# ScalarE's order in the attention slots of a six-block decoder: one move, both exponentials, the other move

## The reference, cut to what matters

```
layer 0:  x = ln(x + attn0(x))                # softmax over a size-1 axis: no attention left
          x = ln(x + xattn0(x, ctx))          # 16 heads, causal, 3x3 filter on the scores  ("near")
          x = ln(x + ffn0(x))                 # MLA attention with rotary keys ("causal"), then 4 experts
layer 1:  x = ln(x + attn1(x))                # 16 heads, causal, plus a memory term          ("tally")
          x = ln(x + xattn1(x, ctx, indices)) # 16 heads over 64 gathered context tokens      ("count")
          x = ln(x + ffn1(x))                 # low-rank experts with running sums

each attention, per head:  s = q k^T (+ mask);  p = exp(s - rowmax(s));  out = (p / sum(p)) v
```

## Time and profile before

| | |
|---|---|
| median of 3 runs | 2637.9 us |
| profiled execution | 2646.27 us |
| its span | 2644.5 us |
| instructions | 38948 |
| granted TensorE clock, mean | 0.876 |
| TensorE busy | 2243.5 us (85%) |
| VectorE busy | 1341.9 us (51%) |
| ScalarE busy | 998.1 us (38%) |

### The profile page before, as it was taken

How to read it: one execution, slowest core, us unless ns; L and a number is a source line. 1 busy time by engine, 2 the same in 40 slices (tenths; PEclk the granted TensorE clock), 3 DMA queues, 4 the chain that set the end, 5 groups by cost and what they waited for, 6 DMA issues and landing times. The chain is left out here.

```text
span 2644.5 us, 38948 instructions
## 1 busy us (share of the span) xinstructions
PE 2243.5 (85%) x13569; PEld 1574.3 (60%) x13637; DVE 1341.9 (51%) x3927; ACT 998.1 (38%) x3145; POOL 363.0 (14%) x639
## 2 busy tenths in 40 slices
PE   8688898898889988896818588899999999999887
PEld 4356566666677755575704355566666666666655
DVE  7245455564645454322129466665656656566331
ACT  3133535343545443352202135453444444444220
POOL 2044141423232324001000000000000000000000
PEclk9768868877899998897958699998999999999888
DMA  8000000000232210344651000000000000000000
GB/s 296 9 4 1 5 5 9 9 5 9 94 104 83 80 31 29 114 162 172 231 135 48 14 10 1 10 5 5 10 5 10 5 10 5 6 5 5 5 1 9
DMA packets 50763, 116.27 MB, mean 44 GB/s; under 512 B 8192, under 2 KB 30464, under 8 KB 46976
## 3 DMA queue, kind: packets, MB, share of 16 engines
q1 hardware_dynamic: 49024, 109.49, 12.3%
q0 software_dynamic: 1536, 4.20, 0.5%
HBM read 90.20 MB, written 23.46 MB: 43 GB/s over the span
## 5 line engine op out<-in xcount | busy, mean ns | idle before, releaser
L690 ACT ACTIVATE PRS<-PT 128x384 f32<-128x384 f32 (+1 forms) x512 | 265.6, 519 | 847.0 <-PE PT L621 846.4
L753 DVE TENSOR_REDUCE negmax<-SM 128x2 f32<-128x512 f32 x432 | 283.9, 687 | 229.1 <-PE SM L584 121.8
L621 PE MATMUL PT<-const_sb,PRS 128*128 128x128 f32 x1664 | 314.2, 307 | 40.0 <-ACT PRS L690 33.9
L705 ACT ACTIVATE PRS<-SM,negmax 128x128 f32<-128x128 f32 x608 | 248.3, 423 | 142.6 <-DVE negmax L753 142.6
L621 PEld LDWEIGHTS PT<-const_sb,PRS 128*128 128x128 f32 x1664 | 210.1, 155 | 134.9 <-issue 101.4
L2756 DVE TENSOR_SCALAR arena<-arena 128x256 bf16<-128x256 bf16 x1024 | 210.5, 281 | 9.2 <-PE SC L2774 8.2
L574 PE MATMUL SM<-haloU,QM 32*128 32x128 f32 (+1 forms) x1056 | 182.2, 388 | 12.0 <-ACT PRS L705 9.5
L574 PEld LDWEIGHTS SM<-haloU,QM 32*128 32x128 f32 x1056 | 136.5, 223 | 27.3 <-ACT PRS L705 13.0
L574 PE MATMUL SC<-haloU,QM 32*128 32x128 f32 (+1 forms) x480 | 120.0, 408 | 34.6 <-ACT PRS L705 34.6
L2774 PE MATMUL SC<-arena,identb 128*128 128x256 bf16 x1024 | 139.1, 279 | 2.7 <-DVE arena L2756 2.7
L636 PE MATMUL OA<-PRS,big 128*32 128x256 f32 (+1 forms) x1024 | 136.5, 393 | 3.0 <-ACT PRS L690 3.0
(11 more groups left out here) (565 smaller groups left out, 4109.9 us busy)
## 6 DMA issues: line engine op xcount, KB each, us to landing
arena<-lay SPq DMA_DIRECT2D x50, 1024.0 KB, 4.9
arena<-lay SPq DMA_DIRECT2D x1, 7700.5 KB, 21.2
rows<-OT SPq DMA_DIRECT2D x2, 3456.0 KB, 31.9
arena<-lay SPq DMA_DIRECT2D x1, 3862.0 KB, 19.9
arena<-rows SPq DMA_DIRECT2D x25, 128.0 KB, 2.8
arena<-lay SPq DMA_DIRECT2D x25, 128.0 KB, 5.3
rows<-arena SPq DMA_DIRECT2D x25, 128.0 KB, 4.6
rows<-OT SPq DMA_DIRECT2D x1, 2432.0 KB, 21.3
```

Of the source, the lines that this page charges most:

```text
L621: ins = pe.transpose(bank[:, o:o + P], PR[n % 4][:, t, k * P:(k + 1) * P], ident)
L690: act.activation(dst, src, ACT.Copy).then_inc(S("probs_moved"), 1)
L705: ins = act.activation(dst, src, ACT.Exp, bias=negmax[:, h, r:r + 1], accum_out=rsum[:, t, h:h + 1])
L753: st.post(dve.tensor_reduce(negmax[:, ORDER[s], :], two(banks[s % NB]), AX.X, ALU.max, negate=True), S("max_ready"))
```

## The change

ScalarE's part of a slot gets another order wherever there is one flip bank and the mode isn't "conv", which is every attention that is executed with these inputs. Before: move of the first turned head, move of the second, exponentials of the two heads of the current pair. Now: move of the first turned head, exponentials of the two heads, move of the second turned head. No instruction is added or removed, no wait changes, and the other four engines' programs are the same. The steps laid beside a slot still come behind all of it.

```
-                early = len(hs.flips) == 1 and mode != "conv"
+                turned = lag <= i < PAIRS + lag
+                single = len(hs.flips) == 1 and mode != "conv"
+                if single and turned:
+                    move_probs(2 * (i - lag))
                 for d in range(2):
                     s = 2 * i + d - ahead
-                    if 0 <= s < H and not early:
+                    if 0 <= s < H:
                         exponentials(s)
-                    if lag <= i < PAIRS + lag:
+                    if not single and turned:
                         move_probs(2 * (i - lag) + d)
-                for s in (2 * i, 2 * i + 1):
-                    if early and s < H:
-                        exponentials(s)
+                if single and turned:
+                    move_probs(2 * (i - lag) + 1)
```

## The result

The changed kernel took 2573.9 us (median of four runs, 2565.5 to 2580.1), beside 2637.1 us for the kernel before (four runs, 2634.8 to 2648.4). The ratio is 0.975, with an interval of 0.971 to 0.979: 63 us or 2.5% faster, where 38 us or 1.4% were forecast. The direction was right, and the size was some 25 us short. The time lies at the low end of the range and close to the smaller case of the rival in which the clock rises (2579 us).

A forecast was written before the change was run, and what follows sets the result against it. TensorE's work and its gaps were taken to bound the kernel, chiefly scores waiting for exponentials. Terms: -50.3 + 2 + 2 + 8 = -38 us from 2637.9, about 2600 us; range 2572 to 2632 us (8 in 10).

The forecast's parts named there:

- the rival in which the clock rises: Layer 0's clock rises with fewer gaps; a fifth of 106 us more gives about 2579 us, half 2547; chance 0.10.
- What bounds the kernel: TensorE, busy 85% of the span, sets the time with its gaps; scores waited 109.8 us for exponentials, the largest item.
- the chain of a slot: Flip, move, both exponentials, scores; without second flip and move, tally loses 1.25 us, causal 1.19, near 0.83, count 1.26.
- The waits that stay: Of 84 score waits, twelve in first slots (16.6 us) and fifteen behind late maxima (28.7 us) stay.
- The cost of the second move: The later second move delays flips: 2 us in causal slots plus 2 us behind last pairs; flips' waits grow some 4 us.
- where the rival had put them: Rival, slower: second move late at each attention's last flip and where maxima are late; about 2654 us, chance 0.07.
- The sum: Attentions: -50.3 us of waits, +2 causal flips, +2 flips behind last pairs, +8 payback, giving -38 us.
- Payback: Closed gaps reopen in chains beside the attentions, such as projection and norm, or at GpSimd's diagonals: about 8 us returns.
- The clock: TensorE's granted clock, left at zero: closing small gaps has no effect on it that the trace could price.
- 50.3 us of waits: Score waits removed: near 14.1 us (18 waits), causal 12.7 (14), tally 11.7 (13), count 11.8 (12).
- the rule: First exponential starts at the later of first move + 0.39 us and first maximum; applied to 84 score waits, removes 50.3 us.

The follow-up runs named there:

- the middle order: Changed kernel, but in near and causal the second move stands between the two heads' exponentials: 2566.9 us, 0.973 of the kernel before.
- near only: Kernel before, with the new order in the eight near attentions alone: 2607.0 us, 0.983 of the kernel before.
- layer 1 only: Kernel before, with the new order in tally and count alone: 2636.1 us, 0.995 of the kernel before.
- fillings: Kernel before, old order, with 174 extra zero-weight matmuls in 21 waits of layer 0: 2607.2 us, 0.986; second version 2602.8 us, 0.987.
- stretch A only: Kernel before, with the new order only in the first seven attentions (near 0 to 3, causal 0 to 2): 2616.9 us, 0.986.
- adding work in dense slots: Changed kernel with its remaining waits filled, plus 3 extra matmuls in each of fifteen other slots of near 0 to 4: 2580.1 us, 0.978.
- causal only: Kernel before, with the new order in the eight causal attentions alone: 2640.4 us, 0.998 of the kernel before.
- filled kernels: Zero-weight matmuls put in TensorE's waits: kernel before (0.986, 0.987), changed kernel (2556.6 us, 0.970), changed kernel with second move between heads (2552.8 us, 0.964).

## Why the prediction was right in direction and short in size

- *What bounds the kernel; the chain of a slot.* Right. The slots shortened as worked out: tally 1.25 forecast and 1.25 where the maximum is in time (0.81 in the slot of rows 4), causal 1.19 and 1.18, near 0.83 and 0.83, count 1.26 and 1.15. The scores' waits fell to 64.5 us, forecast about 60.
- *The waits that stay.* Right: late maxima and first slots kept theirs. In near, VectorE's maximum is what is late next.
- *The cost of the second move.* Mis-sized: flips' waits grew by 15.6 us, not by 4. Six flips of layer 0 with waits of 1.65 to 4.59 us make up 15.1 us of the 49.5. All six stand where the rival had put them, behind the scores of an attention's last pair (five causal, one near). The sum had set 0.3 us for each of seven flips there and nothing for the other 25, since other work stood in front. The rival's mechanism was real, at a few places; with the middle order 9.1 us of it went and the time didn't measurably follow.
- *Payback.* About right in size: in idle time 35.6 us went in all, against the 38 of the sum. By stage 16.1 of 26.8 us of idle time went in layer 0, so 10.7 came back. In layer 1 20.1 of 23.5 went, and 4.2 us of busy time came, which leaves the 15.9 measured.
- *The clock.* This is the step that failed. "The clock is a term that I leave at zero", and "closing small gaps has no effect on it that this trace would let me price", rested on the earlier trace rows: TensorE was busy 18.99 of 20 us at 0.50 and 18.52 at 1.00, so busy share seemed to have nothing to do with the clock. The reading was circular. At the low clock the same work takes longer, so it fills the stretch: the row at 0.50 has 86 matmuls, the one at 1.00 has 160. The busy share was a result of the clock, and said nothing on what came before it. What should have been compared is the same slot at either level, as with near 2's slots 1 and 2 above. The term that was put at nothing measured 30.9 us of busy time in A and 16.4 in B, 47.3 us in this pair of profiles, and 4.2 us the other way in layer 1.
- *The rival "the clock rises".* It had the right mechanism, and its smallest case, a fifth of 106 us, would have given 2579. Against it stood only rows 9, so its chance of 0.10 was too low. Layer 0's attentions ran at 0.84, where there was clock to be won, and 26.8 of the 50.3 us of waits were to go just there. Layer 1, at 0.95, had little to win and won none. That the time came out near the rival's 2579 us owes something to luck, since the fifth in it was a guess.

What is shown: the surplus is clock and lies in layer 0 (stages, near only, layer 1 only); it comes without moving any real work (fillings); it is local (stretch A only); and idle time mostly stands ahead of the clock's falls (35 of 39 in the kernel before). What is argued only: why near's waits weigh more than causal's. What stays open: by which rule the clock falls. Shortening or filling score waits in layer 0 raised it each time, closing waits of flips with the middle order lowered it in A (0.84 to 0.82), adding work in dense slots lowered it once, and adding work where nothing waited raised it in the one execution that was profiled. No theory here foretells all of these.

## What to carry to other kernels

Where the granted clock of a stage is well below 1.00, a closed gap on TensorE can be worth about twice its own length (for 26.8 us by the rule, 63.4 in one pair of profiles and 50 by the ratios of near only and causal only), and at 0.95 only its length less what is paid back (15.9 for 23.5). So price gaps by stage, with the clock of that stage beside them, and keep a term for the clock that isn't zero. Don't read the clock's cause from the busy share of a slow stretch, because the low clock makes that share; compare the same instructions at either level, and count matmuls.

## What the runs showed of the hardware

- 174 matmuls that compute nothing, put into 21 waits, made the kernel 1.3% faster (0.987 [0.981, 0.992]). The granted clock of stretch B went from 0.89 to 0.93. The same number where nothing waited gave 0.999 [0.995, 1.003].
- 45 more in dense slots made it 23.5 us slower, and a slot that got none of them went to the lower level (near 2, slot 2: 8.38 to 11.82 us, 0.49 of it the next slot's extra matmuls).
- Shortening waits of TensorE that were mostly 1.17 to 1.39 us long changed the clock: the near wait of rows 6 was 1.17 us and is 0.34 now, and the new order in near only moved stretch A from 0.77 to 0.81 and the falls in A and B from 39 to 26. The Trainium skill ("TensorE: Matmul & The Clock Gate", section on the psum-queue depth-cycling failure mode) tells of short idle times between groups of matmuls that make the clock go up and down between its two levels; the traces of near only, of stretch A only and of the filled kernels agree with it. Its statement that activity releases the throttle (section on the HAM clock gate) agrees with the same runs, but the kernel with more work in the dense slots of near doesn't: it had more work, and in stretch A a clock of 0.85 instead of 0.88.
- The kernel before varied by 1.4% between executions on one chip (19 runs, 2624.5 to 2661.7); with four executions of a kernel the intervals reach 0.4 to 0.7% to either side, with ten 0.3 to 0.4%.
